# An attention and quantised feed-forward kernel: scores and masks in quarter columns, and the transposes of x and h by VectorE and a trip through DRAM

## What is computed

```python
xn = _layernorm(x, axis=-1)
x = x + _L0_attn_ref(xn, L0_attn_Wqkv, L0_attn_Wout, L0_attn_bout) + _L0_ffn_ref(xn, L0_ffn_w_gate, L0_ffn_w_up, L0_ffn_w_down)
...
    # attention: 16 heads of 16, causal
    dots = jnp.einsum('bhid,bhjd->bhij', q, k) * scale
    dots = jnp.where(causal_mask, -jnp.inf, dots)
    attn = jax.nn.softmax(dots, axis=-1)
    out = jnp.einsum('bhij,bhjd->bhid', attn, v)
...
    # feed-forward: x, h and the weights are rounded to FP4 in blocks of 16
    gate = fp4_linear(x, w_gate)
    y = fp4_linear(x, w_up)
    h = jax.nn.silu(gate) * y
    return fp4_linear(h, w_down)
```

## Time and profile before

| | us |
|---|---|
| median of 3 runs (2761.91 to 2763.21) | 2762.43 |
| the profiled execution | 2762.52 |
| its span, first to last instruction | 2760.8 |
| PE busy | 2562.2 |
| ACT busy | 2038.4 |
| DVE busy | 1934.7 |
| POOL busy | 722.6 |

### The profile page before, as it was taken

How to read it: one execution, slowest core, us unless ns; L and a number is a source line. 1 busy time by engine, 2 the same in 40 slices (tenths; PEclk the granted TensorE clock), 3 DMA queues, 4 the chain that set the end, 5 groups by cost and what they waited for, 6 DMA issues and landing times.

```text
span 2760.8 us, 58289 instructions
## 1 busy us (share of the span) xinstructions
PE 2562.2 (93%) x18228; PEld 1304.5 (47%) x18228; DVE 1934.7 (70%) x5533; ACT 2038.4 (74%) x3502; POOL 722.6 (26%) x550
## 2 busy tenths in 40 slices
PE   2995999999999859999999999999999999999999
PEld 1883444444444424444454444444444445444455
DVE  7995999999999935655645656655656654566555
ACT  1554999999999847777758777775777775777775
POOL 3563334433333221122111112111121111212111
PEclk7997999999999979999999999999999999999999
DMA  2785555555445342202222112123022031220200
GB/s 70 238 272 123 75 75 75 76 72 71 71 70 72 45 84 38 51 19 39 47 78 48 32 31 46 29 58 80 22 42 43 21 76 50 40 47 23 41 24 32
DMA packets 118622, 175.70 MB, mean 64 GB/s; under 512 B 25648, under 2 KB 95024, under 8 KB 117808
## 3 DMA queue, kind: packets, MB, share of 16 engines
q1 hardware_dynamic: 97392, 147.33, 28.6%
q10 hardware_dynamic: 16576, 15.73, 2.1%
q0 software_dynamic: 4352, 8.92, 1.3%
HBM read 129.37 MB, written 42.53 MB: 62 GB/s over the span
## 4 chain that ended last, share of the span: by engine, by line
PE 54%; ACT 4%; issue 4%; SPq 1%; DMA 1%; DVE 0%; ACTq 0%; POOL 0%; DVEq 0%; POOLq 0%
PE O L923 17%; PE S L907 15%; PE F L943 10%; PE F L983 5%; ACT probs L1052 4%; PE F L973 2%; PE S L994 2%; PE S L910 2%; SPq L528 1%; PE F L936 1%; DMA y<-in_L_attn_x_dram 1%; DMA q_st<-s_shift 0%; DVE o_turned L1258 0%; ACTq L1047 0%; ACT xt_hi L1077 0%
## 5 line engine op out<-in xcount | busy, mean ns | idle before, releaser
L1052 ACT ACTIVATE probs<-S 128x1024 f32<-128x1024 f32 (+3 forms) x1280 | 1074.5, 897 | 227.6 <-PE S L910 84.1
L907 PE MATMUL S<-q_st,k_st 128*128 128x512 bf16 (+3 forms) x2560 | 648.8, 351 | 75.0 <-DMA q_st<-s_shift 38.4
L730 ACT ACTIVATE m_excess<-m_DIFF 128x512 f32<-128x512 f32 (+7 forms) x1536 | 647.1, 472 | 88.3 <-PE m_DIFF L690 42.3
L748 DVE CUSTOM_DVE_ANT_0 m_excess<-m_S,m_excess 128x512 f32<-128x512 f32 (+7 forms) x1536 | 700.7, 530 | 11.7 <-PE m_S L690 9.2
L923 PE MATMUL O<-probs,v_sb 128*32 128x512 f32 (+3 forms) x5120 | 603.6, 543 | 2.2 <-POOL v_sb L1129 2.2
L688 PE MATMUL m_S<-m_k,m_q 128*128 128x512 bf16 (+7 forms) x1536 | 483.1, 325 | 26.7 <-DVE m_row_max L748 17.3
L688 PE MATMUL m_DIFF<-m_k,m_q_diff 128*128 128x512 bf16 (+7 forms) x1536 | 478.0, 319 | 29.5 <-DMA m_q_diff<-s_q 29.2
L907 PEld LDWEIGHTS S<-q_st,k_st 128*128 128x128 bf16 x2560 | 213.7, 98 | 418.2 <-ACT probs L1052 235.1
L632 POOL TENSOR_TENSOR m_q_diff<-m_zero,m_q 48x4096 bf16<-48x4096 bf16 x32 | 224.4, 7011 | 429.0 <-DMA m_q<-s_q 418.3
L688 PEld LDWEIGHTS m_S<-m_k,m_q 128*128 128x128 bf16 x1536 | 148.3, 97 | 275.8 <-DVE m_row_max L748 194.9
L1246 DVE TENSOR_TENSOR ht_lo<-F,ht_hi 128x512 fp32r<-128x512 f32 (+1 forms) x128 | 71.0, 557 | 232.5 <-ACT ht_hi L1067 232.5
(11 more groups left out here) (163 smaller groups left out, 4189.8 us busy)
## 6 DMA issues: line engine op xcount, KB each, us to landing
k_st<-s_k SPq DMA_DIRECT2D x96, 256.0 KB, 8.6
q_st<-s_q SPq DMA_DIRECT2D x384, 64.0 KB
s_q<-a_part SPq DMA_DIRECT2D x48, 256.0 KB, 3.0
s_k<-a_part SPq DMA_DIRECT2D x48, 256.0 KB, 2.2
m_q<-s_q SPq DMA_DIRECT2D x96, 128.0 KB, 3.8
m_k<-s_k SPq DMA_DIRECT2D x96, 128.0 KB, 6.7
m_q_diff<-s_q SPq DMA_DIRECT2D x96, 128.0 KB, 8.1
m_k<-s_k SPq DMA_DIRECT2D x96, 124.0 KB, 5.2
```

Of the source, the lines that this page charges most:

```text
L730: act.activation(excess[u % MAX_EXCESS][:, 0:keys // 2], DIFF[u % MAX_BUFS][:, 0:keys // 2], ACT.Relu) \
L748: dve.tensor_tensor_reduce(larger, S[u % MAX_BUFS][:, 0:keys // 2], larger, 1.0, -3e38, ALU.add, ALU.max, column).then_inc(reduced[u % MAX ...
L907: ins = pe.matmul(S[half][:, s % 2, 0:st.width], k_st[p][:, s, st.j * P:(st.j + 1) * P], q_st[st.c % 2][:, s, st.skip:QC], start=True, sto ...
L1052: act.activation(probs[half][st.n % 2][:, :, 0:st.width], S[half][:, :, 0:st.width], ACT.Exp, scale=SCALE).then_inc(exped[half], 1)
```

## The change

- Each score product of 128 output columns becomes four of 32 columns (`quarters`), each into its own quarter of the partitions, as the values' products are; the mask product becomes four, of 32, 64, 96 and 128 queries.
- PE's `x_turn` and `h_turn` are gone. DVE transposes 32x32 blocks (`dve.transpose` into `x_flip` or `h_flip`), SP stores the result to DRAM in one DMA, waits for it, and loads it back in four DMAs (`unflip`) that put the blocks in their places; ACT (`x_high`, `h_high`) and POOL (`x_low`, `h_low`) split it from SBUF.
- The down product of tile n-2 stands at k = 1.
- SP has one list in the order of the steps: the loads of a chunk, then `turn_h` at k = 4, `turn_x` at k = 6. Next batch's first loads are issued at the end of the batch, `v_in` last; POOL places the values behind the first x.
- `FLUSH_DOWN`, the projection before which the last down product stands, is 12, before 6.

```diff
-GATED_AT = {0: ("turn", 0), 2: ("gate", 0), 3: ("up", 0), 5: ("gate", 1), 6: ("up", 1)}
+GATED_AT = {0: ("high", 0), 2: ("gate", 0), 3: ("up", 0), 5: ("gate", 1), 6: ("up", 1)}
...
+def unflip(eng, dst, dram, tiles, sem):
+
+    blocks = dram.rearrange("(a r) (m g s) -> g r m a s", r=SLOT, s=SLOT, g=P // SLOT)
+    for g in range(P // SLOT):
+        rows = dst[g * SLOT:(g + 1) * SLOT, :].rearrange("r (m a s) -> r m a s", m=tiles, s=SLOT)
+        eng.dma_start(rows, blocks[g]).then_inc(sem, 16)
...
+            def turn_h(b, n):
+                sp.wait_ge(q_zeroed, 2)
+                sp.wait_ge(h_flipped, b * tiles + n + 1 + PRIMED)
+                sp.dma_start(dram["h_flip"], h_flip[:, :]).then_inc(h_flip_st, 16)
+                sp.wait_ge(q_zeroed, 2)
+                sp.wait_ge(h_flip_st, b * (16 * tiles) + 16 * (n + 1) + PRIMED)
+                unflip(sp, ht, dram["h_flip"], ITILES, ht_ld)
...
+                for st in steps:
+                    n, k = divmod(st.n, per_tile)
+                    if st.first and st.chunk + 1 < chunks:
+                        load_chunk(b, st.chunk + 1)
+                    if k == 4 and n >= 1:
+                        turn_h(b, n - 1)
+                    elif k == 6 and n + 1 < tiles:
+                        turn_x(b, n + 1)
...
-                    ins = pe.matmul(S[half][:, s % 2, 0:st.width], k_st[p][:, s, st.j * P:(st.j + 1) * P],
-                                    q_st[st.c % 2][:, s, st.skip:QC], start=True, stop=not st.diagonal)
+                    for at in quarters():
+                        ins = pe.matmul(S[half][at, s % 2, 0:st.width], k_st[p][:, s, st.j * P + at.start:st.j * P + at.stop],
+                                        q_st[st.c % 2][:, s, st.skip:QC], start=True, stop=not st.diagonal)
...
-                    if k == 0 and n >= 2:
+                    if k == 1 and n >= 2:
                         down(b, n - 2)
...
+            def h_high(b, n):
+                act.wait_ge(ht_ld, b * (16 * UNFLIP_DMAS * tiles) + 16 * UNFLIP_DMAS * (n + 1) + PRIMED)
+                act.wait_ge(down_ps, b * tiles + n + PRIMED)
+                act.activation(ht_hi[:, :], ht[:, :], ACT.Copy).then_inc(ht_hi_done, 1)
...
+                    if k == 8 and n >= 1:
+                        h_high(b, n - 1)
...
+                def h_turn(n):
+                    dve.wait_ge(h_ready, b * tiles + n + 1 + PRIMED)
+                    dve.wait_ge(ht_lo_done, b * tiles + n + PRIMED)
+                    dve.transpose(h_flip[:, :], h_fp4[:, :]).then_inc(h_flipped, 1)
...
+                    elif k == 4:
+                        if n + 1 < tiles:
+                            x_round_(n + 1)
+                        if n >= 1:
+                            h_turn(n - 1)
```

More of the change, by code:

```diff
@@ new lines, in load_batch @@
+            def load_batch(b):
+                sp.wait_ge(q_zeroed, 2)
+                sp.wait_ge(x_rs, b * tiles + PRIMED)
+                sp.dma_start(norm[:, :, :], dram["norm"][:, bass.ds(b * tiles, tiles), :]).then_inc(norm_ld, 16)
+                sp.wait_ge(q_zeroed, 2)
+                sp.wait_ge(y_head_st, b * 16 + PRIMED)
+                for n in range(HEAD_TILES):
+                    sp.dma_start(y[:, n, :], x_rows[bass.ds(b * T + n * P, P), :]).then_inc(y_ld[n % 2], 16)
+                sp.wait_ge(q_zeroed, 2)
+                sp.wait_ge(v_ready, b * NHG + PRIMED)
+                sp.dma_start(v_in[:, :, :], dram["v"][:, bass.ds(b * NKB, NKB), :]).then_inc(v_ld, 16)
@@ new lines, in batch @@
+            def batch(b, more):
+                turn_x(b, 0)
+                for st in steps:
[6 more added lines that the diff above has]
+                        turn_x(b, n + 1)
+                if more:
+                    load_chunk(b + 1, 0)
+                turn_h(b, tiles - 1)
+                if more:
+                    load_batch(b + 1)
@@ L898, in _ @@
+            load_chunk(0, 0)
+            load_batch(0)
+            with sp.Fori(0, B - 1) as b:
+                batch(b, True)
+            batch(B - 1, False)
         @block.tensor
@@ L925, in values @@
                 ins.then_inc(pv_done, 1)
-            def x_turn(b, n):
-                pe.wait_ge(x_ready, b * tiles + n + 1 + PRIMED)
-                if n == 0:
-                    pe.wait_ge(y_final, b * tiles + PRIMED)
-                else:
-                    pe.wait_ge(gate_free, b * 2 * tiles + 2 * n + PRIMED)
-                if n >= 2:
-                    pe.wait_ge(ht_lo_done, b * 2 * tiles + 2 * (n - 1) - 1 + PRIMED)
-                for kk in range(KD):
-                    ins = pe.transpose(F[0][:, kk * P:(kk + 1) * P], x_fp4[:, kk * P:(kk + 1) * P], ident[:, :])
-                ins.then_inc(xt_ps, 1)
             def gated_product(f, name, ch, done):
@@ L1025, in _ @@
                 for m in range(tiles):
-                    if m == FLUSH_TURN:
-                        for part in range(2):
-                            h_turn(b, tiles - 1, part, flush=True)
-                    elif m == FLUSH_DOWN:
+                    if m == FLUSH_DOWN:
                         down(b, tiles - 1)
@@ L1074, in _ @@
                     exps(b, st, 1)
-                    if op == "turn":
-                        act.wait_ge(xt_ps, b * tiles + n + 1 + PRIMED)
-                        act.activation(xt_hi[:, :], F[0][:, 0:KD * P], ACT.Copy).then_inc(xt_hi_done, 1)
+                    if op == "high":
+                        x_high(b, n)
                     elif op == "gate":
                         gate_parts(b, n, ch)
-                    elif k in (8, 9) and n >= 1:
-                        h_high(b, n - 1, k - 8)
+                    if k == 8 and n >= 1:
+                        h_high(b, n - 1)
                     if k == 9 and n + HEAD_TILES < tiles:
@@ L1085, in _ @@
                         load_tile(b, n + HEAD_TILES)
-                for part in range(2):
-                    h_high(b, tiles - 1, part)
+                h_high(b, tiles - 1)
                 for first, last in STORES:
@@ L1167, in _ @@
                 h_rescale(b, tiles - 1)
+                h_low(b, tiles - 1)
         @block.vector
@@ L1240, in h_round_ @@
                     dve.wait_ge(h_normed, b * tiles + n + 1 + PRIMED)
-                    rounded(h_norm[:, :], fp4_step[:, :], h_rounded)
-                def h_low(n, part):
-                    dve.wait_ge(ht_hi_done, b * 2 * tiles + 2 * n + part + 1 + PRIMED)
-                    lo, hi = (0, 4 * P) if part == 0 else (4 * P, ITILES * P)
-                    dve.tensor_tensor(ht_lo[:, lo:hi], F[part][:, 0:hi - lo], ht_hi[:, lo:hi].bitcast(F32), ALU.subtract) \
-                        .then_inc(ht_lo_done, 1)
+                    rounded(h_norm, fp4_step[:, :], h_rounded)
                 def add_down(n):
@@ L1310, in _ @@
                 for m in range(tiles):
-                    if m == FLUSH_TURN + 1:
-                        for part in range(2):
-                            h_low(tiles - 1, part)
+                    if m == FLUSH_TURN:
+                        h_turn(tiles - 1)
                     elif m == FLUSH_DOWN + 1:
```

160 lines of the change are left out of this document (78 added, 82 removed).

## The result

The changed kernel is slower: 2934.64 us (median of 4 runs, 2925.21 to 2936.97) against 2762.82 for the kernel before on the same chip. The ratio is 1.061, with a 95% interval of 1.059 to 1.064. The forecast was 2807 with a range of 2735 to 2866: the direction was right and the time lies outside the range, by 69 us.

A forecast was written before the change was run, and what follows sets the result against it. PE, busy 93%, was taken as the bound, with ACT a near second. From 2762.5 us, less 67 of gain, plus 92 for late h and 20 for batch edges, came 2807; the 8-in-10 range was 2735 to 2866.

The forecast's parts named there:

- The edges of the batches: Batch ends and starts: 2 us a batch for the last h, 8 us, plus 12 us at starts; 20 us lost.
- x's late copy: ACT's copy of x may be up to 2.3 us late, covered by the down product; priced at nothing.
- The gain: Fewer mode changes and no PE transposes: 1.05 us a tile, 67 us in all, bounds 40 and 83.
- the walk from k = 7 to k = 2: Step-by-step count with ACT as the bound: k = 2 starts at 12.5 us, against 13.2 before.
- changes of mode: Switches between 128-column and 32-column products on PE, read as costing 0.12 and 0.15 us each way.
- h's trip in tiles 0 and 2: h's store queues behind seven q loads, so ACT's copy is 3.3 us late, 28 times: 92 us lost.
- (1): Rival: h's trip is nearly in time, 0.3 us late, giving 2723 us; chance 0.22.
- (2): Rival: small score products have a floor of 0.029 us each, adding 55 us, 2862 us; chance 0.12.
- (3): Rival: products in four quarters run one after the other, scores 3.4 us a step, over 1000 us more; chance 0.02.
- Small terms: DVE's transposes, ACT's copies and POOL's subtractions (some 2.3 us a tile) were expected to lie under PE and ACT.

The follow-up runs named there:

- no_trip_wait: The changed kernel with h and x loaded from the input x, not waiting for the stores, so its result is wrong; 2724.01 us, ratio 0.985.
- copies_later: The changed kernel with ACT's copies of h and x, and POOL's subtraction of h, one step later; 2898.95 us, ratio 1.050.
- trips_mended: The changed kernel with next q loads on ACT's queue, k_st in two bursts, DVE turning x earlier and the old batch-start order; 2817.09 us, ratio 1.020.

## Why the prediction was wrong

The mechanism that the forecast named is there. What failed are other terms of its sum. The edges of the batches were priced at 20 us and cost 60, x's late copy was priced at nothing and cost 27, and two things had no term: PE's stops for instructions (28) and its low clock behind h's waits (some 27).

**The gain: right.** 1.05 a tile was forecast, 1.0 measured (no_trip_wait), and the walk from k = 7 to k = 2 gave 12.5 against 12.53. The stretches with changes of mode came as read: 0.87 apart instead of 0.97 and 1.00.

**h's trip in tiles 0 and 2: the mechanism and nearly the size right, the count not.** By its steps, forecast and then measured at tile 8, in us after k = 4: transpose done 4.8 (4.3), store issued 8.9 (9.7), loads issued 11.6 (12.1), copy 15.8 (16.9), ACT there at 12.5 (12.7). The seven issues took 4.5 us there, where 3.3 were taken (the rows named give 3.1). 28 waits of 3.3, 92 us, were forecast; there are 20 of 3.8 on average, 76.5 us. Tile 14 has no chunk to load after its own (four fewer), and tile 6 was delayed by the instruction stall (four fewer). Tiles 1 and 3 are in time, as forecast.

**x's trip: a step that failed.** "ACT's copy of x may be up to 2.3 late under the down product, its cover; I price it at nothing." ACT waits for x over 0.3 us 32 times, 50.6 us in sum. In tile 1 of each batch there is no down product, since the first stands in tile 2. The timeline there:

```profile
1508.16 0.36 SPq L922 DMA_DIRECT2D s_x_flip<-x_flip  x1
...
1509.87 3.38 SPq L790 DMA_DIRECT2D xt<-s_x_flip  x4
1514.75 0.42 ACT L1095 ACTIVATE xt_hi<-xt 128x256 fp32r<-128x256 f32 x1 [4.30 <-DMA xt<-s_x_flip]
...
1515.49 1.04 PE L967 MATMUL S<-q_st,k_st 128*32 128x512 bf16 x8 [4.15 <-ACT probs L1080]
```

With the low clock behind it, this tile is 6.7 us longer than in no_trip_wait, 27 us in four batches. The other 28 waits are 0.5 to 2 us, nearly all in tiles 0 and 1 and in a batch's tile 2. Where the down product does cover, the forecast was right: at steps 20, 80 and 120 the step is 0.8 to 1.8 us longer than in no_trip_wait, and the next one is shorter by as much. A cover has to be named for every tile, the first ones too.

**The edges: the largest miss.** 20 us were forecast. Between batches 27 us are lost and 5 at the end, and a batch's first tile is 7.1 us longer than before, 28 in all: 60. Of these the wait at step 4 alone is 13.8. The trip of the last h has nothing beside it, and the down product waits for it after the twelve projections ahead of it are used up. PE's timeline (the 1.90 us of its last row are not new: before, the same place had 1.5 to 1.7):

```profile
1944.94 0.58 PE L1018 MATMUL F<-w_down_hi,ht_hi 128*128 128x256 f32 x1 [4.48 <-POOL ht_lo L1159]
...
1955.19 0.40 PE L967 MATMUL S<-q_st,k_st 128*32 128x512 bf16 x4 [1.90 <-issue]
```

The forecast's 2 us a batch counted the trip's length against projections. It left out that q's loads for step 4 had moved behind x's first trip on SP.

**Not in the forecast at all: the stalls for instructions,** 18.5 us by the profile and 28 with what follows them (though removing them alone gave at most 5), **and the clock after a wait.** After the stall at 2147 PE's values take 2.19 us and not 1.03, at a granted clock of 0.50, the lower of the two levels (1.2 GHz). The same is seen behind h's wait in tile 8, in stretches as above:

```profile
2214.50:2219.00 4.50, 0.31 (x4) 0.00 (x0) 0.00 (x0) 1.52 (x3) 0.60 (x1) 1.00 0.57 105
2219.00:2223.30 4.30, 4.04 (x81) 2.29 (x81) 2.66 (x5) 2.38 (x6) 2.63 (x3) 0.62 0.33 62
```

What it costs can be read where PE and ACT wait for nothing new: step 30, two steps behind h's late copy, takes 3.5 to 3.7 us at a granted clock of 0.54 to 0.58, and 2.2 in no_trip_wait at 1.00. So a wait of 3 to 4 us costs 1.3 to 1.5 us more than it lasts. Over the whole run the mean granted clock is 0.952 against 0.978.

**The account,** by the steps of the two profiles. no_trip_wait has a span of 2722.1 us: 2760.8 - 63.1 (gain) + 13.6 (batch starts) + 7.8 (between batches and the end) + 3.0 (ahead of the first batch). The changed kernel adds 82 in tiles 2, 4, 8, 10 and 12 of the batches (h), 27 in tiles 3, 5, 9, 11 and 13 behind them (the low clock, and in three of them what x's short waits add), 27 in tile 1 (x), 28 in tile 6 and at step 104 (instructions), 15 in tile 0 (q at step 4 and the first x), 1 in the other tiles and 24 between batches and at the end, less 2 ahead of the first batch. That is 2924, and 2923.5 was measured.

**The rivals.** (1) A trip in time was put at 2723, and no_trip_wait gives 2724. That this is so near is luck: 8 us of lateness were allowed and there are none, and the gain was 4 smaller and the edges 4 larger than assumed. The chance of 0.22 was for something that the order on SP excluded. (2) A floor of 29 ns under small products is denied: 32 start in 0.41 us. The Trainium skill (TensorEngine Tiling (Array Packing), "Instruction Overhead") has about 60 cycles for each matmul, as much as 60 columns; an estimate from that figure is 0.8 us for 32 products. For products in different quarters this case's rows speak against it. (3) is denied by the 0.87. Small terms: DVE's transposes take 0.97 and 0.43 us (1.05 and 0.36 forecast), ACT's copies 0.85 and 0.42 (0.75 and 0.28), and POOL's subtractions 1.8 and 0.7 a tile (2.3 together were forecast, though the row named gives 2.0).

## What to carry to other kernels

A step that leaves a busy engine for an idle path is free only if its result is there when the next engine comes for it. Write down the deadline and the queue position for every tile kind, the first and last of a loop too, and count every transfer ahead of it on the same queue and every one in flight beside it. Where a few cases can't be in time, leave those on the old path: every kernel that computes with the trips and beats the one before has a batch's first x and last h on PE and the copies a step later. How much each of the two is worth, no run tells apart; between batches, where later copies alone give nothing (copies_later has +29 there), it is 19 us against trips_mended. And test the parts of a change apart: here one was a gain of 17 us that the other buried.
